# Two 64-wide heads' scores side by side: queries without the zero half, upper and lower 64 rows issued together

## What is computed

```python
# layer 0 (n=0) and layer 3 (n=3), 16 heads of width 64, per batch
q = layernorm(x) @ Wq                      # 256 x 1024
k, v = split(context @ Wkv)                # 256 x 1024 each
sim = (q * scale) @ k.T                    # per head 256 x 256
# layer 0: masked keys get -inf (one mask for all batches)
# layer 3: one more "null" key and value per head; mask by key
attn = softmax(sim); out = attn @ v
x = x + out @ Wo                           # layer 3: normed once more
...
# layer 1: 16 heads of width 8; layer 2: 8 heads of width 128
```

## Time and profile before

| what | value |
|---|---|
| median of three runs | 1949.45 us |
| profiled execution, its span | 1948.2 us |
| PE busy | 1760.2 us, 90% |
| DVE busy | 1222.4 us, 63% |
| ACT busy | 966.7 us, 50% |
| matmuls of `kT` and `Qz` (all layers) | 1568 records, 442.3 us |
| one `mid` batch of layer 0 (281.98 to 329.63 us) | 47.65 us |
| one `mid` batch of layer 3 (1685.49 to 1739.52 us) | 54.03 us |

### The profile page before, as it was taken

One profiled execution on the slowest core, in us unless ns is written; L12 is line 12 of the kernel. 1 busy time (PEld: TensorE's weight loads), 2 busy tenths in 40 slices (PEclk: granted clock), 3 DMA queues, 4 the chain that ended last, 5 costly groups with the idle time before them and its releaser, 6 DMA issues.

```text
span 1948.2 us, 40574 instructions
## 1 busy us (share of the span) xinstructions
PE 1760.2 (90%) x14281; PEld 1350.1 (69%) x14281; DVE 1222.4 (63%) x3198; ACT 966.7 (50%) x2010; POOL 265.7 (14%) x358
## 2 busy tenths in 40 slices
PE   4999999989997899988999977999968999999987
PEld 3788888866664688875777754666646777777775
DVE  5966666667665678884222246555555778777781
ACT  1566666654332567775444343323314556555552
POOL 2000000011002143321000014000010011111111
PEclk9999999999998899998999989999978999999999
DMA  8000000000002000000000010000000000000000
GB/s 251 1 1 0 0 0 0 0 2 1 1 0 64 27 1 0 0 1 1 1 1 0 0 51 1 1 1 0 0 0 1 1 1 0 0 0 0 0 1 22
DMA packets 19157, 21.09 MB, mean 11 GB/s; under 512 B 4650, under 2 KB 14003, under 8 KB 18884
## 3 DMA queue, kind: packets, MB, share of 16 engines
q1 hardware_dynamic: 19076, 20.02, 3.6%
HBM read 18.97 MB, written 1.05 MB: 10 GB/s over the span
## 4 chain that ended last, share of the span: by engine, by line
PE 65%; DVE 18%; ACT 7%; issue 7%; POOL 1%; SPq 1%; DMA 0%; DVEq 0%; ACTq 0%; POOLq 0%
PE bank L1152 56%; PE bank L1156 9%; DVE PTs L1754 2%; DVE negm L1745 2%; DVE negm L1750 2%; ACT Pm L1053 2%; DVE Qz L1949 2%; ACT VxF L1010 1%; ACT PTs L1009 1%; ACT Pm L1113 1%; DVE Qz L1549 1%; DVE VxF L604 1%; DVE st L1557 1%; DVE On L1810 1%; SPq L699 1%
## 5 line engine op out<-in xcount | busy, mean ns | idle before, releaser
L1152 PE MATMUL bank<-kT,Qz 128*128 128x256 f32 (+1 forms) x1568 | 442.3, 387 | 4.0 <-issue 1.6
L1053 ACT ACTIVATE Pm<-bank,negm 128x256 f32<-128x256 f32 x784 | 326.7, 468 | 207.0 <-DVE negm L1750 206.3
L1152 PE MATMUL bank<-xH,R 128*128 (+3 forms) x928 | 299.6, 382 | 13.5 <-DVE Qz L1949 13.4
L1152 PEld LDWEIGHTS bank<-R,Qz 128*128 128x128 f32 (+1 forms) x2496 | 293.8, 192 | 17.8 <-ACT Qz L1120 6.4
L1152 PE MATMUL bank<-R,Qz 128*128 128x128 f32 (+1 forms) x2496 | 295.2, 276 | 3.1 <-ACT Qz L1120 3.1
L1152 PEld LDWEIGHTS bank<-kT,Qz 128*128 128x128 f32 x1568 | 248.9, 192 | 67.9 <-issue 16.9
L1156 PE MATMUL bank<-ident,Pm 128*128 128x128 f32 x1568 | 239.1, 275 | 50.6 <-DVE PTs L1754 40.6
L1754 DVE TENSOR_TENSOR PTs<-bank,PTs 128x512 f16<-128x512 f32 x384 | 261.9, 682 | 7.7 <-ACT PTs L1009 7.2
L1156 PEld LDWEIGHTS bank<-ident,Pm 128*128 128x128 f32 x1568 | 187.2, 141 | 113.3 <-issue 59.2
L1750 DVE TENSOR_REDUCE negm<-bank 128x2 f32<-128x512 f32 x264 | 181.6, 688 | 95.6 <-PE bank L1152 91.7
L1009 ACT ACTIVATE PTs<-bank 128x512 f16<-128x512 f32 (+1 forms) x388 | 231.3, 596 | 3.1 <-PE bank L1156 3.1
(11 more groups left out here) (231 smaller groups left out, 2085.1 us busy)
## 6 DMA issues: line engine op xcount, KB each, us to landing
R<-in_L_ffn_ew SPq DMA_DIRECT2D x2, 1024.0 KB, 6.9
R<-in_L_ffn_w SPq DMA_DIRECT2D x1, 2048.0 KB, 9.8
R<-in_L_xattn_Wkv SPq DMA_DIRECT2D x2, 768.0 KB, 6.5
R<-in_L_ffn_w SPq DMA_DIRECT2D x1, 1408.0 KB, 12.9
R<-in_L_xattn_Wq SPq DMA_DIRECT2D x2, 512.0 KB, 3.7
out<-x SPq DMA_DIRECT2D x4, 256.0 KB, 2.3
PTs<-in_ctx SPq DMA_DIRECT2D x1, 768.0 KB, 8.1
R<-in_L_xattn_Wo SPq DMA_DIRECT2D x1, 512.0 KB, 7.8
```

The source lines that it names most:

```text
L1053: last = act.activation(Pm[:, k % 4, qt * S:(qt + 1) * S], bank[k % 2][:, qt * S:(qt + 1) * S], ACT.Exp, bias=negm[:, k % 4, qt:qt + 1])
L1152: return pe.matmul(o, l, r, start=start, stop=stop)
```

## The change

Queries are stored as keys are, two heads to a slot: `Qz[:, k // 2, :]`, features of the even head on partitions 0 to 63, of the odd one on 64 to 127. One move reads a `q` fill out, and both settings to zero are gone. For heads of width 64 the step `scores` is replaced by `pair`, which stands at even i only and makes the scores of heads i and i+1: one mask matmul of 512 columns for each of banks 0 and 1, then four matmuls over 64 partitions, in the order (first half of the queries, even head), (first half, odd head), (second half, even head), (second half, odd head). Even heads go to bank 0, odd ones to bank 1. Each head's last matmul counts `scores`. The pair waits until `exp` has counted head i-1, since it writes both banks. The other steps, their order and their waits stay as they are.

```diff
--- before.py
+++ after.py
@@ -110,8 +110,12 @@
 OWN = [("q", 3), ("k", 3), ("v", 1), ("v", 3)]
 
 
-def head_steps(i):
-    st = [("scores", i), ("softmax", i)] if i < 16 else []
+def head_steps(i, paired):
+    st = []
+    if i < 16 and paired:
+        st = ([("pair", i)] if i % 2 == 0 else []) + [("softmax", i)]
+    elif i < 16:
+        st = [("scores", i), ("softmax", i)]
     st += [("turn", i - 2)] if i < 18 else []
     st += [("low", i - 3)] if i < 19 else []
     st.append(("av", i - 4))
@@ -126,7 +130,7 @@
     table = WIDE_NULL if A.null else WIDE if A.pieces >= 8 else NARROW
     st = []
     for i in range(A.nh):
-        st += [(kind, k) for kind, k in head_steps(i) if k >= 0 or not first]
+        st += [(kind, k) for kind, k in head_steps(i, A.dh == 64) if k >= 0 or not first]
         for step in table.get(i, []):
             if step in PREVIOUS:
                 if not first:
@@ -155,7 +159,7 @@
 
     st = []
     for i in range(16, 20):
-        st += [(kind, k - 16 if kind != "norm" else k - 8) for kind, k in head_steps(i)]
+        st += [(kind, k - 16 if kind != "norm" else k - 8) for kind, k in head_steps(i, A.dh == 64)]
         if i == 17 and A.dh == 64:
             st.append(("outT", -2))
     st.append(("outT", -1))
@@ -615,7 +619,7 @@
         kTall = kT[:, :, :].rearrange("p h s -> p (h s)")
 
         def keys_of(A, b, h):
-            return kT[:, h // 2, :] if A.dh == 64 else kTall[:, bass.ts(b, S)] if A.n == 1 else kT[:, h, :]
+            return kTall[:, bass.ts(b, S)] if A.n == 1 else kT[:, h, :]
 
         def bank_of(n):
             return bank[6 + n % 2]
@@ -654,10 +658,7 @@
 
         def att_evac(A, move, kind, k, b, kinds, src):
             if kind == "q" and A.dh == 64:
-                Q4 = Qz[:, :, :].rearrange("p (g u) s -> p g u s", u=2)
-                v = src[:, :].rearrange("p (g s) -> p g s", s=S)
-                move(Q4[0:64, 2 * k:2 * k + 2, 0, :], v[0:64], A.scale)
-                return move(Q4[64:128, 2 * k:2 * k + 2, 1, :], v[64:128], A.scale)
+                return move(Qz[:, 2 * k:2 * k + 2, :].rearrange("p h s -> p (h s)"), src[:, :], A.scale)
             if kind == "q" and A.n == 1:
 
                 return move(xnT[:, k * 512:(k + 1) * 512], src[:, :], A.scale)
@@ -801,7 +802,6 @@
                                     base=0, pattern=[[-8, 16]], channel_multiplier=1))
             link(pool.affine_select(out=headmask[:, :], in_=headmask[:, :], compare_op=ALU.is_ge, fill=0.0,
                                     base=7, pattern=[[8, 16]], channel_multiplier=-1))
-            pool.memset(Qz[:, :, :], 0.0)
             pool.memset(On[:, :, 1024:1152], 0.0).then_inc(consts_ready, 1)
 
             def normalise(n, stats_sem, value, yn_sem, scale, offset, chain, at=0):
@@ -851,8 +851,6 @@
                     pool.wait_ge(vmax3_rows, 1)
                     pool.partition_all_reduce(vmaxall[:, 3:4], vmax[:, 3:4], P, RMAX).then_inc(vmax3_max, 1)
 
-                    need(pool, ffn_s[2].stats, NCH)
-                    pool.memset(Qz[:, :, :], 0.0)
                     pool.wait_ge(prep3_rows, 1)
                     pool.partition_all_reduce(amx, am, P, RMAX).then_inc(prep3_max, 1)
 
@@ -1326,10 +1324,28 @@
                 def body(b, kinds):
                     nh = A.nh
                     for kind, k, m, base in steps(A, b, kinds):
-                        if kind == "scores":
-                            if k == 0 and kinds in ("single", "first"):
-
-
+                        if kind == "pair":
+                            if k == 0 and kinds == "first":
+                                fills_read(b, m)
+
+                            need(pe, s.exp, b * nh + k)
+                            for u in range(2):
+                                o = bank[u][:, :].rearrange("p (q s) -> p q s", s=S)
+                                if A.mask == "full":
+                                    mm(o, identb[:, :], mb0[:, :, :], True, False)
+                                else:
+                                    mm(o, onesb[:, :], mb3[:, bass.ts(b, S)].unsqueeze(1).to_broadcast([P, 2, S]),
+                                       True, False)
+                            for qt in range(2):
+                                for u in range(2):
+                                    rows = slice(64 * u, 64 * u + 64)
+                                    last = mm(bank[u][:, qt * S:(qt + 1) * S],
+                                              Qz[rows, k // 2, qt * P:(qt + 1) * P], kT[rows, k // 2, :],
+                                              False, qt == 1)
+                                    if qt == 1:
+                                        last.then_inc(s.scores.sem, 1)
+                        elif kind == "scores":
+                            if k == 0 and kinds == "single":
                                 fills_read(b, m)
                             if A.n == 1 and k % 4 == 0:
                                 need(pe, s.qm, b * 4 + (k // 4 + 1))
@@ -1337,11 +1353,7 @@
                             need(pe, s.exp, b * nh + (k - 1))
                             for qt in range(2):
                                 o = bank[k % 2][:, qt * S:(qt + 1) * S]
-                                if A.mask == "full":
-                                    mm(o, identb[:, :], mb0[:, qt, :], True, False)
-                                elif A.mask == "key":
-                                    mm(o, onesb[:, :], mb3[:, bass.ts(b, S)], True, False)
-                                last = mm(o, Qz[:, k, qt * P:(qt + 1) * P], keys_of(A, b, k), A.mask is None, True)
+                                last = mm(o, Qz[:, k, qt * P:(qt + 1) * P], keys_of(A, b, k))
                             last.then_inc(s.scores.sem, 1)
                         elif kind == "turn":
                             need(pe, s.exp, b * nh + (k + 1))
```

## The result

The changed kernel takes **1987.57 us**, median of 4 runs (1985.58 to 1990.42), against 1950.0 (1949.03 to 1950.72) of the kernel before: a ratio of **1.0195, 95% interval 1.018 to 1.0209**, so slower, by about 2%. 1987.0 was predicted.

The account below looks back on a forecast made before the run. PE was taken to bound layer 0, PE with DVE close behind layer 3; +4.8 us in layer 0 and +32.9 in layer 3 on a span of 1948.2 gave 1985.9, plus 1.25 for the median: 1987, range 1945 to 2075.

Parts of the forecast that it names:

- between two pairs the whole chain must run: Attention: scores, two maxima with `low` between, and exponentials run between pairs, 5.42 us in layer 3, 4.5 in layer 0.
- PE work alone decides: Rival, both layers' attention: the chain stays hidden, 42 us less, 1907 us; chance 7%.
- no overlap: Rival, pair's scores: eight passes one after another, a pair of 2.48 us, 2067 us in all; chance 20%.
- pair by pair walk: Walk through PE, DVE and ACT lists: batches of 58.06 us against 54.0 in layer 3, 47.67 against 47.9 in layer 0.
- if starts stay in order: Pair's scores: only one head's second pass overlaps the other's first, so five passes of 0.215 us, 1.08.
- change of shape: PE, each pair: going from 128 rows to 64 and back costs 0.33 us, between ends of 0.19 and 0.57.
- 0.1 us of a pair moves the time by 12.3: Sensitivity, both layers: a pair costing PE 0.1 us more or less moves the time by 12.3 us.
- the rival of four passes: Rival, pair's scores: full overlap, a pair of 1.62 us, -7.5 and +20.9 us, 1963 in all; chance 12%.
- break-even of 1.53: Pair's PE cost: the kernels before and after are level at a pair of 1.53 us.
- first and last: Layer 0's first and last batches: maxima ahead of a softmax and block moves, +5.9 us together.
- The clock falls: Rival, layer 3: PE's gaps lower its clock to 0.85, +34 us, 2021 in all; chance 10%.
- the two zeroings: POOL's zeroing of the queries: removal brings nothing, a few us at most in the preparation.

Follow-up runs that it names:

- e2_zero_half: Changed kernel with its pair step and wait, but queries stored with the zero half and matmuls over all 128 rows: 2037.18 us.
- e1_apart: Changed kernel with new storage and 64-row matmuls, but each head by itself in the order and with the waits of the kernel before: 1999.37 us.
- e5_early_mask: Changed kernel with bank 0's mask waiting only for head i-2's exponentials, bank 1's still for head i-1's: 1971.68 us.
- e7_two_places: Changed kernel with layer 3's `v 3` moved behind head 5's softmax, `v 2` and `resid2` behind head 13's: 1961.96 us.
- e9_old_tables: Kernel before, heads one at a time and zeros stored, with tables of steps spread anew for its own order: 1915.87 us.
- e3_by_head: Changed kernel with the four score matmuls reordered: both query halves of the even head, then both of the odd: 1986.8 us.
- e11_ln: Changed kernel with bank 0's mask waiting for its own head alone and new step tables, layer 0's remade with layer norm's transposes at head 14: 1900.42 us.

## Why the prediction was right, and where it was not

**The main step held: between two pairs the whole chain must run.** It is shown from three sides: the wait alone costs 87 us (`e2_zero_half`), without it layer 3 is faster than with it (`e1_apart`, 56.18 against 58.09 a batch), and 0.22 us less in it bring 16 us (`e5_early_mask`). The starts in it came as walked: DVE at 1.70 us (1.68), the odd maximum at 3.33 (3.30). The rivals *PE work alone decides* and *no overlap* fall.

**The pair by pair walk held in its places.** Layer 3, forecast 5.6, 5.6, 8.0, 10.9, 6.1, 6.1, 9.2, 6.5; measured in the batch from 1702.14 5.78, 5.60, 7.89, 11.74, 6.15, 6.17, 9.03, 6.39, where 11.74 holds the stretch of lower clock. An undisturbed batch is 58.09 against 58.06. The waits of 2.9, 2.1 and 1.6 us in front of heads 6, 14 and 0 are 2.67, 1.71 and 1.39. That `v 3` makes the first is shown by `e7_two_places`: the third period falls from 7.89 to 5.69, and in an undisturbed batch no wait for exponentials is over 1.4 us. With `v 2` and `resid2` moved as well, the seventh falls only from 9.03 to 8.66, for PE then waits 1.8 us there for ACT's side of a bank, and a wait of up to 1.4 in front of head 0 stays.

**The overlap was mis-sized: four passes, not five.** The step that failed is "if starts stay in order". Four units of 0.215 are 0.86 instead of 1.08. The change of shape is 0.35 us, near the 0.33 that was taken: 0.10 from the last mask's columns to the first pass, 0.10 more from the first two passes to the next, 0.10 from the last pass to the first transpose and 0.05 more from this to the next. Together the pair is 1.65, not 1.84. By distances between starts, 128 pairs thus take 67 us less of PE (0.52 each) and not 42. The page's busy time fell by 36 only; it counts whole records, so also the ends of matmuls that now run out ahead of a gap, and those at the lower clock.

**This miss cost almost nothing, and that shows a second fault.** The text said that 0.1 us of a pair moves the time by 12.3, and that the rival of four passes gives 1963. With 0.19 us less, 23 us should have been won. The same walk with 1.65, but with the place at which each head's scores end as the trace has it, gives 33 us over before, nearly as with 1.84 (this is worked out, no run shows it): with five units the even head ended at 1.68 and the odd one later, with four both end at 1.70, and DVE takes the even one first in either case. The sensitivity had let the end of the even head's scores move with the whole pair. DVE's start at 1.70 us is in the trace, and 1.68 was the forecast. Where the chain decides, only the part of the pair ahead of that point counts; the rival of four passes was priced wrong, and so was the break-even of 1.53.

**Layer 0 was put too high, layer 3 too low.** Layer 0: six mid batches of 47.12, 3.2 us won and not 1.1, probably because its chain is shorter and there the cheaper pair tells, which no run shows apart; first and last about +5.0, against +5.9. Layer 3: +38.7 to the last `wo` against +32.9; up to 4.4 of the difference is the lower clock. The rival *The clock falls* did come, as stretches of 3.4 us behind the long gaps, but as 4 to 7 us and not 34: it had been priced as a lower clock throughout.

**Outside the attentions, one term was put at nothing and was not.** The prediction gave the two zeroings "nothing, and a few us at most in the preparation". In layer 3's preparation the second one had held up DVE. Before, and then the same cast in the changed kernel:

```profile
1441.39 3.58 POOL L855 MEMSET Qz<- 128x4096 f32 x1
1442.18 2.84 DVE L1680 CAST VxF<-vscale 128x16 f16<-128x16 f32 x1
```

```profile
1442.69 0.20 DVE L1692 CAST VxF<-vscale 128x16 f16<-128x16 f32 x1
```

Before, a cast of 16 columns took 2.84 us and ended as POOL's zeroing did; without the zeroing it takes 0.20. It is 2.84 or 2.85 in `e2_zero_half` and `e9_old_tables` too, which have the zeroing, and 0.20 in `e1_apart`, `e3_by_head` and `e11_ln`, which do not. The cast stands in the chain ahead of layer 3, so 2.6 us are won there. Of the 1.1 us between the layers little else is of the change: the last `wo` of layer 0 runs at half clock in the changed kernel and at full clock before (its matmuls 0.21 us apart instead of 0.11, +2.9), and other stretches of lower clock fall elsewhere. Of the 2.6 us ahead of layer 0's first mask, about 1.1 are of the single moves of `q` (one of 604 ns for the two halves of 590 in the earlier trace rows, on DVE one of 0.68 us for two that took 1.38), 0.3 lie ahead of both, and about 1.2 come from the clock, which rose to full at 36.8 us instead of 39.6. Nothing in the edit bears on that, so it may be chance.

```profile
L1007 ACT ACTIVATE Qz<-bank 128x512 f32<-128x512 f32 x3 | 1.8, 604 | 3.7 <-PE bank L1150 3.7
```

The forecast of 1987 is right in total to 1 us because 6.6 us too much for layer 0 with what lies around it and 6.4 too little for layer 3 and the tail cancel. That is luck; by its own steps the forecast is right to some 6.

## What to carry to other kernels

Before two steps are joined so that they share a resource, write down what each waited for, and what the joint one waits for: here a wait for head i-2 became one for head i-1, and a chain of maxima and exponentials that had lain beside PE's work set the pace. What the join saves is then had only if the order around it is made anew; the same order that hid nearly everything before put two steps into the middle of the chain after. And test such tables on the old kernel too: most of the gain of the paired kernel with new tables, 34 of 50 us, needed no pairs. The other 16 are not all of the pairs either: that kernel also has the mask wait of `e5_early_mask`, and a layer 0 table that was mended a second time.

## What was not expected of the hardware

- In these traces f32 matmuls in the upper and the lower 64 rows run fully beside each other, their passes 7 to 13 ns apart, also when all of one half stand ahead of all of the other in the program.
- A change from 128 rows to 64 and back costs 0.35 us here with f32 weights: 0.20 on the way in, 0.15 on the way out.
- While POOL zeroed 4096 columns (3.58 us), a DVE cast of 16 columns from f32 to f16 took 2.84 us instead of 0.20; three DVE instructions of one column in the same time took 0.15 to 0.21, as without the zeroing.
- Work that is not needed made a kernel faster: 12 masks a batch in PE's gaps, 21 us of work in all, took 6.7 us off; PE's clock then stayed at 2.4 GHz in layer 3. A stretch of 3.4 us at 1.2 GHz made a batch 0.6 to 1.6 us longer.
